# A graph-attention layer over a sparse adjacency: the key-bias product on GpSimd, its sum on ScalarE, and five blocks of x loaded ahead

## The reference

```python
q = x @ Wq.T + bq
k = key @ Wk.T + bk
v = value @ Wv.T + bv
scores = einsum('nd,md->nm', q, k) / N ** 0.5
adj_scores = scores * adj
adj_scores = where(abs(adj_scores) < 1e-05, -1e9, adj_scores)
prob = softmax(adj_scores, axis=-1)
y = einsum('nm,md->nd', prob, v) @ Wm.T + bm
out = layernorm(x + y, axis=-1)
```

## Time and profile before

| | |
|---|---|
| median of 3 runs | 447.91 us (447.75 to 448.69) |
| the profiled execution | 449.37 us |
| its span, from first to last instruction | 447.6 us |
| busy: TensorE, VectorE, ScalarE, GpSimd | 432.1, 315.8, 190.3, 168.7 us |
| bytes moved by DMA | 121.58 MB, 272 GB/s over the span |
| key bias on VectorE | 35 products of 0.743 us and 35 readouts of 0.082 us |

### The profile page before, as it was taken

The page is one execution under the profiler, slowest core; times in us unless marked ns, Lnnn a source line. Parts: engine busy times, 40 slices in busy tenths (PEclk is TensorE's granted clock), DMA queues, the critical chain, the costliest instruction groups (busy, mean ns, idle before and its releaser), DMA issues.

```text
span 447.6 us, 5475 instructions
## 1 busy us (share of the span) xinstructions
PE 432.1 (97%) x1536; PEld 245.7 (55%) x1536; DVE 315.8 (71%) x923; ACT 190.3 (43%) x448; POOL 168.7 (38%) x180
## 2 busy tenths in 40 slices
PE   8999999899999999999999999999999999999982
PEld 5344444344444456566666666666566656666651
DVE  0347525698439647787888889888879878847675
ACT  1233422323333243434445454554545445464573
POOL 3100000000425118463655656547205776174300
PEclk9999999989999999999999999999999999999997
DMA  8999999999999999987899999999949879568333
GB/s 324 369 236 276 294 287 288 227 244 240 284 321 331 343 307 257 299 306 234 252 299 261 325 317 326 339 346 304 299 169 302 256 227 364 168 187 292 108 142 115
DMA packets 32452, 121.58 MB, mean 272 GB/s; under 512 B 5080, under 2 KB 5336, under 8 KB 30370
## 3 DMA queue, kind: packets, MB, share of 16 engines
q0 software_dynamic: 16240, 72.79, 61.1%
q1 hardware_dynamic: 12866, 28.51, 17.6%
q10 hardware_dynamic: 3312, 19.89, 11.3%
HBM read 139.78 MB, written 17.56 MB: 352 GB/s over the span
## 4 chain that ended last, share of the span: by engine, by line
PE 76%; issue 10%; DMA 6%; DVE 4%; ACT 3%; POOL 1%; POOLq 0%; DVEq 0%; ACTq 0%
PE bank L574 24%; PE bank L564 14%; PE bank L682 12%; PE bank L720 12%; PE bank L664 6%; DMA big<-adj_tiles 6%; PE bank L615 3%; PE bank L693 2%; PE bank L673 2%; PE bank L608 1%; ACT keyT L893 1%; ACT y_buf L951 1%; DVE stats L1277 1%; POOL big L462 1%; DVE big L1057 1%
## 5 line engine op out<-in xcount | busy, mean ns | idle before, releaser
L574 PE MATMUL bank<-big,M 128*128 128x472 f32 (+1 forms) x288 | 121.9, 550 | 0.3 <-ACT y_buf L838 0.3
L564 PE MATMUL bank<-y_buf,big 128*128 128x512 f32 x256 | 113.3, 602 | 0.7 <-ACT y_buf L860 0.7
L481 POOL DMA_INDIRECT v_g<-table,index x70 | 71.9, 1027 | 80.8 <-PE bank L720 51.9
L471 POOL DMA_INDIRECT key_adj_g<-key_adj,index x70 | 73.3, 1046 | 49.7 <-DVE index L1145 29.0
L564 PEld LDWEIGHTS bank<-y_buf,big 128*128 128x128 f32 x256 | 48.7, 192 | 60.5 <-issue 59.0
L574 PEld LDWEIGHTS bank<-big,M 128*128 128x128 f32 x288 | 51.9, 190 | 46.0 <-issue 43.8
L1057 DVE TENSOR_TENSOR big<-big 128x1888 bf16<-128x1888 bf16 x35 | 39.8, 1137 | 52.9 <-DMA big<-adj_tiles 52.9
L682 PE MATMUL bank<-keyT,qT 128*118 128x256 f32 x280 | 66.3, 380 | 0.7 <-ACT keyT L893 0.7
L462 POOL DMA_DIRECT2D big<-adj_tiles x35 | 19.9, 568 | 124.5 <-PE bank L564 82.0
L720 PE MATMUL bank<-v_g,probT 128*118 128x512 f32 x136 | 64.0, 593 | 0.5 <-ACT probT L930 0.5
L682 PEld LDWEIGHTS bank<-keyT,qT 128*118 128x118 f32 x280 | 50.8, 182 | 22.6 <-issue 10.9
(11 more groups left out here) (122 smaller groups left out, 469.8 us busy)
## 6 DMA issues: line engine op xcount, KB each, us to landing
big<-adj_tiles POOLq DMA_DIRECT2D x35, 944.0 KB, 14.6
x_buf<-x SPq DMA_DIRECT2D x35, 256.0 KB, 7.4
out<-y_buf SPq DMA_DIRECT2D x34, 256.0 KB, 5.5
big<-valueT ACTq DMA_DIRECT2D x8, 1024.0 KB, 11.3
big<-xT SPq DMA_DIRECT2D x7, 944.0 KB, 10.6
table<-qT ACTq DMA_DIRECT2D x5, 1024.0 KB, 14.6
table<-y_buf ACTq DMA_DIRECT2D x3, 1024.0 KB, 16.0
big<-xT ACTq DMA_DIRECT2D x2, 944.0 KB, 8.6
```

The lines of the kernel that those rows point to most:

```text
L471: pool.indirect_dma_start(key_adj_g[:, b, c, :], None, key_adj, bass.IndirectOffsetOnAxis(index[:, t, CH + c:CH + c + 1], 0),).then_inc(ke ...
L481: pool.indirect_dma_start(v_g[:, b, c, :], None, table, bass.IndirectOffsetOnAxis(index[:, t, c:c + 1], 0), bounds_check=N - 1, oob_is_err ...
L564: mm = nc.tensor.matmul(bank[4 + t % 2][:, :], col_buf[nb % 2][:, d, k * P:(k + 1) * P], G[:, d, :], start=(d == 0), stop=(d == DC - 1))
L574: mm = nc.tensor.matmul(ps[:, 0:n], M[:, d, a * P:(a + 1) * P], xT_buf[nb % 2][:, d, 0:n], start=(d == 0), stop=(d == DC - 1))
```

## The change

Three edits go together. The loads of x ahead of the loop are cut from seven to five; in the loop block i + 5 is loaded in turn i, behind the stores and the transposed x of that turn. The dot product leaves VectorE: GpSimd multiplies a block of x with w into one of three new buffers, three tiles ahead (three products in front of the waits for the stored table, then one in each turn between the gather of values and the adjacency loads). ScalarE then sums each product, in turn i that of tile i + 1, behind the copy of the transposed weights and ahead of the copy of the query unit. kappa is brought in as kappa / 512 added to each of the 512 numbers, for which VectorE makes one column, `kappa_part`, once.

```diff
+CB = 3
+XAHEAD = 5
+        kappa_part = sb("kappa_part", [P, 1])
-        c_prod = big[0:P, 13952:14464]
+        c_prod = sb("c_prod", [P, CB, D])
+        c_prod_sb = sem("c_prod_sb")
+        kappa_sb = sem("kappa_sb")
 # SyncE
-            for t in range(XB):
+            for t in range(XAHEAD):
                 load_x(t)
             for i in range(T + 1):
                 for t in finish_of(i - 1):
                     store(t)
                 if i % 4 == 0 and i // 4 + 2 < QBL:
                     load_xT(i // 4 + 2)
-                if i >= 1 and i + XB - 1 < T:
-                    load_x(i + XB - 1)
+                if i + XAHEAD < T:
+                    load_x(i + XAHEAD)
 # GpSimd
+            def bias_product(t):
+                pool.wait_ge(x_in[t % XB], 16 * (t // XB + 1))
+                if t == 0:
+                    pool.wait_ge(prep_sb, 2 * DC + 2)
+                if t >= CB:
+                    pool.wait_ge(c_sb, t - CB + 1)
+                nc.gpsimd.tensor_tensor(c_prod[0:R, t % CB, :], x_buf[0:R, t % XB, :], w_row[0:R, :], ALU.mult
+                                        ).then_inc(c_prod_sb, 1)
             for i in range(3):
                 for t in trees_of(i):
                     load_adj(t)
+            for t in range(CB):
+                bias_product(t)
             pool.wait_ge(spare_sb, VD)
...
                 if i >= 2 and i + VD - 2 < T:
                     gather_values(i + VD - 2)
+                if i + CB < T:
+                    bias_product(i + CB)
                 for t in loads_of(i):
                     load_adj(t)
 # ScalarE
+            def bias_sum(t):
+                act.wait_ge(c_prod_sb, t + 1)
+                if t == 0:
+                    act.wait_ge(kappa_sb, 1)
+                nc.scalar.activation(c_prod[0:R, t % CB, :], c_prod[0:R, t % CB, :], ACT.Identity, bias=kappa_part[0:R, 0:1],
+                                     accum_out=c_cols[0:R, t:t + 1]).then_inc(c_sb, 1)
+            bias_sum(0)
             for i in range(T + 1):
...
                 if i < T:
                     copy_prob(i)
+                if i + 1 < T:
+                    bias_sum(i + 1)
                 u = q_unit(i)
                 if u is not None:
                     copy_q(u, bank[7])
 # VectorE
-            def key_bias(t):
-                dve.wait_ge(x_in[t % XB], 16 * (t // XB + 1))
-                if t >= 1:
-                    dve.wait_ge(c_sb, t)
-                nc.vector.tensor_tensor_reduce(c_prod[0:R, :], x_buf[0:R, t % XB, :], w_row[0:R, :], 1.0, kappa[0:R, 0:1],
-                                               ALU.mult, ALU.add, accum_out=c_cols[0:R, t:t + 1]).then_inc(c_sb, 1)
             def bias_columns():
+                dve.wait_ge(prep_sb, 2 * DC + 1)
+                nc.vector.tensor_scalar(kappa_part[:, :], kappa[:, :], 1.0 / D, None, ALU.mult).then_inc(kappa_sb, 1)
...
             value_sums()
-            dve.wait_ge(prep_sb, 2 * DC + 2)
-            key_bias(0)
             reduce_tile(FIRST - 1)
...
-                if t < T - 1:
-                    key_bias(t + 1)
```

## The result

The changed kernel takes 468.01 us (median of 4, 466.44 to 469.29) against 447.84: a ratio of 1.0445, 95% interval 1.0426 to 1.0465. The forecast was 451.7 us with a range of 448.4 to 454.2. The direction was right, the size was not: +20.2 us came where +3.8 were expected.

What follows compares the result with a forecast made beforehand. TensorE, busy 97% of the span, was taken to bound the kernel. Front gain used up (-0.1), clock fall (+1.77) and tail sums (+2.13) made +3.8 us: 451.7 us, range 448.4 to 454.2.

Steps and rivals of the forecast that it cites:

- VectorE's relief is worth nothing: Loop and tail: taking 35 products with their sums, 0.743 us each, from VectorE brings nothing back; price 0.
- A sum costs 0.71 us, hidden in the loop, 2.13 us in the tail: ScalarE: a sum fits its 1.23 us idle in the loop; those of tiles 32 to 34 add 2.13 us.
- The idle before the count shrinks to 0.49 us and the clock holds: Table stage: TensorE's 1.98 us wait for VectorE's count falls to 0.49, saving 1.49 plus 1.77 of clock loss: 3.26 us.
- Two transfers can't follow; 0.9 us survive: Front: an adjacency load comes only 1.57 us earlier, tile 0's second value gather no earlier; at most 0.9 us survives.
- faster: Rival: both transfers follow TensorE, products do not hinder; the front's 3.26 us reach the loop: 446.8 us; chance 0.08.
- A product takes 1.0 us (0.44 to 1.32): Length of one product on GpSimd, against 0.743 us on VectorE; 1.0 us taken, bounds 0.44 and 1.32.
- The first three alternate with VectorE and delay it by 2.25 us: Ahead of the loop: first product costs VectorE's chain 0.25 us, the others 1.0 each; TensorE idles 3 us, clock falls, +1.77.
- In the loop the waits added cost nothing: Loop: GpSimd's products run three tiles ahead; loads and gathers queued behind them are used tiles later, so price nothing.
- this case: The main forecast, with GpSimd's first three products hindering VectorE: 451.7 us, 449.8 to 453.0; chance 0.38.
- The products come too late: Rival: the sums, and with them the masking, wait for GpSimd in every tile; over 454 us; chance 0.04.

Runs made afterwards that it cites:

- half dummies: Kernel before plus 35 unread GpSimd multiplications of 256 columns in place of 512, at the places of the products: 451.96 us, ratio 1.0081.
- 35 dummies: Kernel before plus 35 unread GpSimd multiplications of 512 columns at the places of the products, key bias still on VectorE: 463.94 us, ratio 1.0373.
- first three alone: Kernel before plus only three unread GpSimd multiplications, those ahead of the loop: 452.1 us, ratio 1.0085.
- the 17: Kernel before plus 17 unread GpSimd multiplications, only in loop passes in which VectorE reduces no adjacency tile: 449.76 us, ratio 1.0033.

## Why the prediction was wrong

Step by step, as it was put:

- *VectorE's relief is worth nothing*: right. Leaving the key bias out altogether gives 446.8 us against 446.44.
- *A sum costs 0.71 us, hidden in the loop, 2.13 us in the tail*: right. It lasts 712 ns, the loop stays level with it, and with all 35 on ScalarE the span grows by 2.1 us (447.0 against 444.9); without the last three sums it is 444.6.
- *The idle before the count shrinks to 0.49 us and the clock holds*: right, 0.51 and 1.00 with the x blocks alone. The price of the clock, 1.77 us, was taken from one profiled execution and added to the median of all. Half of the profiles with seven blocks ahead have no such fall, and the times gained 1.5 us where the profiled spans gained 2.7: the term was too large for the median.
- *Two transfers can't follow; 0.9 us survive*: wrong. Of the 3.3 us at tile 0, 3.0 are still there at tile 34 with the x blocks alone. I read from the earlier trace rows how long each transfer took, but not what its issue waited for: the adjacency load waits for TensorE and so moved with it by 3.3 us, and the second gather, behind a first one that waits for the stored table, went out at 165.24 us in place of 168.19. The rival "faster" had this outcome, at 0.08, but for another reason: that the engines lose less to the two blocks at their new place.
- *A product takes 1.0 us (0.44 to 1.32)*: 1.28, near the upper end. The estimate of 1.12 from the Trainium skill's "GPSIMD Engine Reference" (section 3.1) was nearer, still too short.
- *The first three alternate with VectorE and delay it by 2.25 us*: wrong. One pass waited for all three, 3.78 us longer. TensorE then idled 3.40 us (3 predicted), which is luck in part: without the products VectorE's chain ended 2.9 us earlier than before (2.3 put), and they delay it by 3.8 (2.25 put). The clock did not fall there in the profiled run of the kernel after; it did with the products and sums alone, after an idle of 3.41. These are both rows of TensorE's timeline with the window behind, the kernel after first:

```profile
162.11 1.12 PE L718 MATMUL bank<-keyT 128*128 128x512 f32 x2 [3.40 <-DVE keyT L1217]
...
164.00:168.00 4.00, 4.00 (x19) 2.44 (x18) 3.09 (x5) 2.44 (x5) 1.56 (x2) 1.00 1.02 211
```

```profile
164.81 2.05 PE L717 MATMUL bank<-keyT 128*128 128x512 f32 x2 [3.41 <-DVE keyT L1216]
...
164.00:168.00 4.00, 3.19 (x4) 1.49 (x5) 1.03 (x2) 1.10 (x3) 0.00 (x0) 0.61 1.02 227
```

- *In the loop the waits added cost nothing*: **the step that failed.** Between tiles 4 and 30 the kernel after loses 11.2 us. I looked at what is queued behind the product on GpSimd and priced the hindrance between GpSimd and VectorE only for the first three products, where I had a timeline before me. The same hindrance meets VectorE at most of the other 32: by the timeline 23 of them lie over an instruction of VectorE that lasts 0.6 to 1.8 us longer than it does elsewhere. Where VectorE reduces a tile and works almost without a pause, such a hold goes straight into TensorE's wait for the weights, 14.7 us in place of 3.4. Rows 12 held the hint: the one VectorE operation that I had found stretched beside GpSimd's gathers, L1253, is one of those that the products hold.

The parts of the profiled 17.1 us, by the table: -2.9 for the x blocks and the kept clock (the kernel without GpSimd's products at tile 0), +3.7 for the first three products (from -2.9 to +0.8), +13.0 between tiles 0 and 30 (all of it in the loop, where the kernel without them stays level), +2.3 from tile 30 to tile 34, where the three sums alone take 2.2 (some of it may be held passes), +1.0 after the last absolute value, with the slow last matmuls.

The range of this case does not quite follow from its terms either: with products of 1.32 and sums of 0.80 they give 452.8, not 453.0.

No rival named this. "The products come too late" had the size, over 454 us, but another mechanism: ScalarE waited 2.2 us for products in the whole kernel.

## What to carry to other kernels

Before arithmetic goes to GpSimd, list VectorE's instructions with two inputs in SBUF, and its TENSOR_SCALAR passes from SBUF to SBUF (L1258, L1271), and take each product as a hold of up to its whole length on whichever of them it meets (MAX8, MATCH_REPLACE8 and the batch-norm statistics, also from SBUF, were not held here); what matters is VectorE's slack at that place, not its share of busy time. Relief is worth something only if the relieved engine is late: leave the work out altogether once, and the run gives the ceiling (here none). And to say whether a transfer moves along, ask what its issue waits for, not only how long it takes.

## What the runs showed of the hardware beyond that

- A held instruction shows in the trace as a long one, not as idle time: 0.15 us of work recorded as 1.89. Shares of busy time rise where an engine stands still (VectorE 326.2 us busy, with 26 us of work less).
- Products in a row are not interleaved with a waiting VectorE instruction: it stood through all three, 3.78 us beyond its length.
- Who waits can't be read from the recorded starts: at 192.59 in the kernel after the first reduction pass began 0.40 us ahead of a product of 512 columns and stood (2.69 us for 1.13); at 200.86 with the half dummies it began 0.40 us ahead of one of 256 columns and ran (1.33), while GpSimd stood (1.41 for 0.63). Why is left open; recorded spans on GpSimd are rough.
- Equal idles of TensorE were followed by different clocks: 2.72 us at the same place and time by a granted clock of 1.00 with the 35 dummies and a fall with the first three alone; 3.40 and 3.41 us by 1.00 and 0.61; 1.72 us in the tail by 0.53 in the kernel after and by 1.00 in the one with the product on VectorE; before the count 2.06 us by 1.00 with the 35 dummies and 1.82 by 0.50 with the 17. The length of the idle alone did not tell in these runs. So a price for the clock read from one profile holds for that execution, not for the median.
